# Pair-interaction recommender tower: VectorE takes over the copies of the transposed fields, SyncE their second copies, and the batched units are spaced anew

## The reference

```python
e = jnp.stack([tbl_f[ids[:, f]] for f in range(40)], axis=1)   # 512 x 40 x 64
...
vi, vj = e[:, i_idx, :], e[:, j_idx, :]                        # all 780 pairs i < j
z = einsum('bpe,bpe->bp', einsum('bpd,pde->bpe', vi, W), vj)   # W is 780 x 64 x 64
h = jnp.concatenate([z, dense_ctx], axis=1)                    # 512 x 796
h = jnp.maximum(h @ W_top1 + b_top1, 0.0)                      # 512 wide
h = jnp.maximum(h @ W_top2 + b_top2, 0.0)                      # 256 wide
y = h @ W_top3
```

## Time and profile before

| quantity | value |
|---|---|
| median of 3 runs | 354.84 us (354.65 to 357.09) |
| profiled execution | 354.51 us, of which 352.3 us are the span from the first to the last instruction |
| TensorE, VectorE busy | 316.6 us, 250.2 us |
| GpSimd, ScalarE busy | 233.1 us, 219.1 us |

### The profile page before, as it was taken

How to read it: one execution, slowest core, us unless ns; L and a number is a source line. 1 busy time by engine, 2 the same in 40 slices (tenths; PEclk the granted TensorE clock), 3 DMA queues, 4 the chain that set the end, 5 groups by cost and what they waited for, 6 DMA issues and landing times.

```text
span 352.3 us, 5566 instructions
## 1 busy us (share of the span) xinstructions
PE 316.6 (90%) x1472; PEld 112.1 (32%) x1472; DVE 250.2 (71%) x252; ACT 219.1 (62%) x1696; POOL 233.1 (66%) x194
## 2 busy tenths in 40 slices
PE   0799865999959899999889999999999969999997
PEld 0133423333223333332223333333233323333442
DVE  2375782888728788989759999999999959940000
ACT  1001200467979779779969898897999979600032
POOL 6777777777777767753883899799894953920000
PEclk9999996999989999999989999999999989999999
DMA  6733452333322327632122411423311200000000
GB/s 170 229 105 93 111 146 56 87 97 107 86 58 89 86 79 262 199 95 69 47 75 60 110 45 57 117 64 97 83 41 55 60 0 1 2 0 2 0 0 0
DMA packets 17865, 27.66 MB, mean 79 GB/s; under 512 B 4901, under 2 KB 5029, under 8 KB 17834
## 3 DMA queue, kind: packets, MB, share of 16 engines
q1 hardware_dynamic: 9770, 17.86, 16.9%
q0 software_dynamic: 4608, 4.73, 6.1%
q10 hardware_dynamic: 3456, 4.72, 4.7%
HBM read 22.57 MB, written 0.00 MB: 64 GB/s over the span
## 4 chain that ended last, share of the span: by engine, by line
PE 44%; ACT 25%; POOL 11%; DVE 7%; issue 6%; ACTq 4%; DMA 1%; DVEq 0%
ACT batched L371 24%; PE ps_t L538 18%; PE ps_t L521 8%; PE ps_z L560 7%; POOL rows L319 6%; PE ps_t L586 5%; DVE prod L446 5%; POOL wide_rows L319 5%; ACTq L355 4%; PE ps_t L621 2%; PE ps_e L586 2%; DVE batched L460 2%; PE ps_e L500 1%; ACT E L348 1%; DMA rows<-in_tbl,ids_sb 1%
## 5 line engine op out<-in xcount | busy, mean ns | idle before, releaser
L371 ACT ACTIVATE batched<-batched 128x64 f32<-128x64 f32 x832 | 198.8, 242 | 40.0 <-DVE batched L460 16.6
L446 DVE TENSOR_TENSOR prod<-ps_t,E 128x1024 f32<-128x1024 f32 x148 | 170.9, 1216 | 29.5 <-PE ps_t L538 27.5
L371 ACT ACTIVATION_READ_ACCUMULATOR batched<-batched 128x1 f32 x832 | 156.5, 188 | 0.0
L538 PE MATMUL ps_t<-E,w_sb 64*128 64x512 f32 x592 | 147.4, 621 | 5.5 <-ACT E L348 3.4
L319 POOL DMA_INDIRECT rows<-in_tbl,ids_sb x128 | 121.3, 948 | 38.1 <-issue 37.8
L326 POOL TENSOR_TENSOR prod<-prod 128x1024 f32<-128x1024 f32 x40 | 93.6, 2371 | 32.8 <-DVE prod L446 32.6
L538 PEld LDWEIGHTS ps_t<-E,w_sb 64*128 64x128 f32 x592 | 51.6, 187 | 89.7 <-issue 55.7
L460 DVE TENSOR_TENSOR batched<-ps_t,wide_rows 128x1024 f32<-128x1024 f32 x52 | 60.4, 1218 | 19.4 <-PE ps_t L521 19.2
L521 PE MATMUL ps_t<-w_sb,E 64*128 64x512 f32 x208 | 51.5, 637 | 8.2 <-issue 8.2
L560 PE MATMUL ps_z<-prod,quads 128*32 128x512 f32 x352 | 52.6, 611 | 0.0
L348 ACT ACTIVATE E<-ps_e 128x512 f32<-128x512 f32 x18 | 10.5, 583 | 41.1 <-PE ps_e L489 22.7
(11 more groups left out here) (41 smaller groups left out, 60.8 us busy)
## 6 DMA issues: line engine op xcount, KB each, us to landing
w_sb<-in_w_units SPq DMA_DIRECT2D x50, 256.0 KB, 2.7
E<-E ACTq DMA_DIRECT2D x72, 64.0 KB, 2.1
rows<-in_tbl,ids_sb POOLq DMA_INDIRECT x128
w_sb<-in_w SPq DMA_DIRECT2D x7, 256.0 KB
prod<-in_ids_by_field SPq DMA_DIRECT2D x2, 512.0 KB, 9.1
prod<-in_tbl SPq DMA_DIRECT2D x3, 312.5 KB
w_sb<-in_w SPq DMA_DIRECT2D x1, 512.0 KB
wide_rows<-in_tbl,ids_sb POOLq DMA_INDIRECT x16, 4.3
```

The lines of the kernel that those rows point to most:

```text
L371: last = act.activation(products, products, ACT.Copy, accum_out=zt[:, b, at:at + 1])
L446: dve.tensor_tensor(prod[:, n % P_RING, s, :, :], ps_t[:, step % STEPS, :, :], multiplier, ALU.mult).then_inc(product_ready, 1)
L538: last = pe.matmul(ps_t[:, step % STEPS, j, :], w_sb[at:at + DIM, m % W_RING, col:col + P], E[at:at + DIM, slot_of(pairs_of(n)[s][j]), :], ...
```

## The change

`BATCHED` and `BATCHED_AT` are new numbers: pairs k = 14 and 12 lose their batched unit, 13 and 11 get one; units stand at least three apart. Pairs u = 6 and 7 are turned directly ahead of the first group that uses them. From u = 6 on the copy out of `ps_e` is VectorE's, in its place in `order()`, and the four placing DMAs are SyncE's, between its weight loads (for u = 12 behind the parameter loads). ScalarE keeps u = 0 to 5 and all sums.

```diff
-BATCHED = (14, 12, 10, 9, 8, 7, 6, 5, 4, 3, 2, 1, 0)
-BATCHED_AT = (4, 6, 10, 13, 17, 20, 24, 27, 31, 34, 38, 41, 45)
+BATCHED = (13, 11, 10, 9, 8, 7, 6, 5, 4, 3, 2, 1, 0)
+BATCHED_AT = (3, 7, 11, 14, 18, 21, 24, 28, 31, 35, 38, 42, 45)
...
 def ahead(u):
-    return 1 if u < 12 else 2
+    return 0 if u in (6, 7) else 1 if u < 12 else 2
...
+BY_SCALAR = 6
...
+        def place_fields(eng, u):
+
+            k = KP - 1 - u
+            if k < 2:
+                return
+            eng.wait_ge(e_copied, place(u) + 1)
+            for f in range(2):
+                for h in range(2):
+                    to, of = (2 * (k % 2) + f) * HALF, f * DIM + h * HALF
+                    eng.dma_start(E4[to:to + HALF, k // 2 - 1, h, :], E[of:of + HALF, slot_of(k), :]).then_inc(
+                        e4_placed[u], 16)
...
             for kind, at in order():
-                if kind == "fields" and at == PARAMS_AT:
-                    load_params()
+                if kind == "fields":
+                    if at == PARAMS_AT:
+                        load_params()
+                    if at >= BY_SCALAR:
+                        place_fields(sp, at)
...
+                act.activation(E[:, u, :], e_bank[u], ACT.Copy).then_inc(e_copied, 1)
+                place_fields(act, u)
...
-                if kind == "fields" and at >= FIRST:
+                if kind == "fields" and FIRST <= at < BY_SCALAR:
                     copy_fields(at)
...
+            def copy_fields(u):
+                dve.wait_ge(product_ready, last_step(u - E_RING) + 1)
+                dve.wait_ge(e4_placed[u - E_RING], 64)
+                dve.wait_ge(transposed, u - LOOKED_UP + 1)
+                dve.tensor_copy(E[:, u % E_RING, :], e_bank[u]).then_inc(e_copied, 1)
...
             for kind, at in order():
-                if kind == "batched":
+                if kind == "fields" and at >= BY_SCALAR:
+                    copy_fields(at)
+                elif kind == "batched":
                     multiply_batched(at)
```

More of the change, by code:

```diff
@@ L339, in copy_fields @@
             def copy_fields(u):
-                k = KP - 1 - u
                 if u < LOOKED_UP:
```

## The result

The changed kernel takes 341.89 us (median of 4 runs, 341.62 to 342.54) against 355.68 us in the same runs of the kernel before: ratio 0.9612, 95% interval 0.957 to 0.9655, so 3.9% faster. The forecast was 343 us. The profiled execution took 342.54 us with a span of 340.7 us, 11.6 us less than the span before.

The account below looks back on a forecast made before the run. Late ScalarE copies, then TensorE and VectorE together, bound the middle; the start waited for gathered rows, with GpSimd late next. 354.5 less 8.0 up to group 35 and 3.3 behind it, tail unchanged, gave 343 us; range 337 to 349.

Parts of the forecast that it names:

- add 21: GpSimd's add that the sum behind group 27 needs; forecast to end at 139.6 us, losing only GpSimd's 2.75 us wait.
- group 35 through on VectorE: VectorE's last step of group 35 ends at 173.5 us, 1.3 after TensorE, instead of 181.5: gain 8.0 us.
- ScalarE leaves the chain: Without fourteen copies and twelve pairs' DMA issues on ScalarE, TensorE's waits of 4.91, 2.53 and 3.31 us go.
- The gate: At the sum behind group 27 TensorE comes some 5 us early and stands until GpSimd's add ends at 139.6.
- the front: Stretch up to the sum behind group 27, reached at 133 to 135 us; pairs 6 and 7 drain, about 2 us each.
- The low clock: After TensorE's wait at the sum behind group 27, a granted clock of 0.50 costs 1.4 us extra.
- Behind group 35: From group 35 to the last product: 127.7 us instead of 131.0, five copies at 0.60 each included; gain 3.3 us.
- the rival in which no copy finds a gap: All eight VectorE gaps behind group 35 but the last stay, giving 130.1 us there and 346 total; chance 0.12.
- SyncE: SyncE takes 48 placing DMA issues at 0.4 us each, 1.6 us a pair; cost to the kernel nothing.
- drain at every pair: Rival: each copy between turning and first group empties the pipeline, 2.1 us instead of 0.60; 359 us, chance 0.07.
- Copies don't stop GpSimd: Opposed rival: seven VectorE copies at 0.68 us stop GpSimd, making it 4.8 us later; 348 us, chance 0.05.
- No wait for add 21: Rival: no 5 us wait at the sum behind group 27, or no low clock after it; 338 us, chance 0.12.

Follow-up runs that it names:

- run 7: Changed kernel, but ScalarE issues all placing DMAs while VectorE still copies: 342.06 us, ratio to the kernel before 0.9604.
- run 8: Changed kernel, but ScalarE copies all pairs while SyncE still issues the placing DMAs: 341.24 us, ratio to the kernel before 0.9577.
- run 10: Kernel before in its old order, ScalarE copying all pairs, with only the placing DMAs from pair 6 on moved to SyncE: 339.98 us against 355.67.
- run 3: Changed kernel, but GpSimd does not add the halves of groups 20 and 21; TensorE sums them in sixteen passes: 336.33 us.
- run 4: Changed kernel, but pairs 6 and 7 are turned one group ahead again, as before: 342.74 us.
- run 5: Changed kernel, but VectorE copies each of pairs 6 to 12 a second time, to a spare tile: 340.87 us.
- run 1: Kernel before in its old order, with copies moved to VectorE and placing DMAs to SyncE: 339.82 us, ratio 0.9566.
- run 6: Changed kernel, but VectorE copies each of pairs 13 to 19 a second time, to a spare tile: 345.38 us.
- run 11: Changed kernel, but GpSimd adds groups 34, 35, 58, 59, 72, 73 instead of 20 and 21; alters the computation, timing only: 334.65 us.
- run 12: Changed kernel with GpSimd adding groups 34, 35, 58, 59, 72, 73 instead of 20, 21, and ScalarE making all copies; alters the computation: 330.91 us.
- run 2: Kernel before with only the new order (batched units, places, turning of pairs 6 and 7); ScalarE copies and issues: 349.19 us.

## Why the prediction was right

| step | forecast | measured |
|---|---|---|
| VectorE copies pair 6 | 58.7 | 58.9 |
| TensorE through with group 27 | 133 to 135 | 135.5 (131.84 + 3.63) |
| add 21 ends | 139.6 | 139.1 |
| TensorE's wait there | about 5 | 3.69 |
| sum and batched unit at low clock, extra | 1.4 | 2.6 |
| group 35 through on VectorE | 173.5 | 174.8 |
| from there to the last product | 127.7 | 126.1 |
| tail | 39.8 | 39.8 |

*ScalarE leaves the chain.* Right (0%). Runs 7, 8 and 10 add what the forecast did not say: in ScalarE's queue the issues weigh more than the copies (29 against 8 us), and moving them alone is enough; in the new order so is moving the copies alone.

*The gate.* This was the step on which the number hung. TensorE came later and waited less than forecast, since the clock fell behind the drain of pair 7 (5.23 us for a couple of 3.70). Run 7, where it did not fall there, shows what was forecast:

```profile
70.04 3.70 PE L552 MATMUL ps_t<-E,w_sb 64*128 64x512 f32 x16 [2.30 <-issue]
...
139.52 1.94 PE L574 MATMUL ps_z<-prod,quads 128*32 128x512 f32 x8 [5.51 <-POOL prod L341]
```

That error vanished in the wait, as the prediction said such errors would. Runs 3, 4 and 5 show the gate from three sides: take it away and 5.6 us come back; make the front 6.9 us later and 0.9 are lost; load VectorE with 4.2 us ahead of it and nothing is lost. Run 1 shows the other side: where TensorE comes behind the add, there is no wait.

*The low clock* was sized too small by 1.2 us: the sum took 141.09 - 139.23 = 1.86 instead of 1.00, and the batched unit 146.57 - 141.09 = 5.48 instead of 3.75. But TensorE also went on 0.4 us earlier than forecast and was 0.5 us quicker from pair 13 to group 35, so it was through at 172.5, against 172.2. The 1.3 us by which group 35 came late are for the greater part VectorE's: its last step ended 2.3 us behind TensorE's last product, not 1.3. The 1.3 was the distance in the kernel before, where TensorE had just waited for ScalarE and VectorE had only two steps to do; now it did four in a row, at 1.15 us each.

*Behind group 35* the gain was 4.9 us instead of 3.3. Three gaps of 0.87 us remained at batched units, 2.6 us against the 3.5 that were put in; the other 0.7 us lie in the work (123.5 us instead of 124.2). The copies did fit behind the turning: by run 8 they cost at most 0.26 us each, under the 0.60 taken, and only a second copy (run 6) comes near it. So the rival in which no copy finds a gap did not come true. The Trainium skill (Perfetto Trace Analysis, Optimizing Scalar/DVE Operations) says that offloading work from a saturated VectorE to ScalarE may make sense. Run 8 gives 0.65 us for it, which is not settled, and runs 11 and 12 give 3.7 us once the gate is out of the way, most of it in the front.

*SyncE.* Its issues took 0.59 us each, not 0.4; nobody waited for them. The changed kernel's placing DMAs, by issuing engine (ns min/median/max):

```profile
L275 SPq DMA_DIRECT2D E<-E x48: 507/591/1086, 62.1 to 225.6; - x48
L275 ACTq DMA_DIRECT2D E<-E x24: 514/612/617, 25.4 to 50.0; - x24
```

*The rivals.* No drain at every pair (345.38 in run 6, not over 348). Copies don't stop GpSimd: gather instructions beside them took 0.94 to 0.96 us, and all forty adds, several of them beside a copy, 2.35 to 2.39 us. "No wait for add 21" described run 3, not the change.

The errors of +1.3 and -1.6 us nearly cancel, and the 343 owes that to luck. Another -0.4 lies around the span (1.8 us instead of 2.2), and the median is 0.65 us below the profiled execution.

## What to carry to other kernels

An engine that is late with a short step may be relieved of something else in its queue: here moving 48 DMA issues was worth as much as moving the copies and the issues together (runs 10 and 1). Before counting a gain in front of an in-order queue on another engine, work out when that queue would be through without any waits, since what comes earlier than that is lost. A reordering that helps against one limit should be tried again, with and without it, each time a limit is gone: here the new order gave about 6 us alone, cost about 2 beside the moved work, and gave about 4 without the gate.

## What the hardware showed that was not expected

The length of a wait did not settle what TensorE's clock did behind it. Windows behind a wait, granted clock in the third column from the end. In the changed kernel, behind 2.30 us for the copy of pair 7 and 3.69 us for add 21:

```profile
70.05:73.00 2.95, 2.95 (x8) 1.51 (x10) 0.77 (x1) 2.95 (x27) 2.34 (x3) 0.50 0.42 100
...
139.20:143.00 3.80, 3.77 (x14) 1.11 (x16) 0.00 (x0) 0.00 (x0) 2.85 (x3) 0.50 0.09 17
```

In run 7 behind the same 2.30 us, then in run 5 behind 3.19 us for add 21:

```profile
70.04:73.00 2.96, 2.96 (x14) 1.55 (x16) 1.73 (x2) 0.54 (x5) 2.27 (x3) 1.00 0.34 89
```
```profile
139.70:144.00 4.30, 4.30 (x24) 1.56 (x24) 2.08 (x2) 0.82 (x7) 3.39 (x4) 1.00 0.11 21
```

0.50 is the level of 1.2 GHz, 1.00 that of 2.4. In run 2 the clock was 1.00 behind a wait of 2.82 us and 0.50 behind one of 2.95. Where it fell, it cost 1.5 us (at pair 7) and 2.6 us (at add 21). What decides between the two stays open here. Run 5, with more work ahead of the gate, was 1.0 us faster than the changed kernel by the medians; that the clock is the cause is likely, but the two were not timed together.
